# A recurrent stage with three gates of input first, one round ahead, and an ODE loop without work behind its branch

## The reference, cut to what matters

```python
def _mlp(y, W1, b1, W2, b2, W3, b3):
    h = jnp.tanh(y @ W1.T + b1)
    h = jnp.tanh(h @ W2.T + b2)
    return h @ W3.T + b3

def _rk4_step(y, dt, params):
    k1 = f(y)
    k2 = f(y + dt / 2 * k1)
    k3 = f(y + dt / 2 * k2)
    k4 = f(y + dt * k3)
    return y + dt * (k1 + 2 * k2 + 2 * k3 + k4) / 6
...
def _lstm_activate(gates, c):
    i, f, g, o = jnp.split(gates, 4, axis=-1)
    c_new = jax.nn.sigmoid(f) * c + jax.nn.sigmoid(i) * jnp.tanh(g)
    h_new = jax.nn.sigmoid(o) * jnp.tanh(c_new)
    return (h_new, c_new)

def step(carry, x_t):
    h, c = carry
    sel_in = jnp.concatenate([h, c, x_t], axis=-1)
    logits = sel_in @ W_sel.T + b_sel
    onehot = jax.nn.one_hot(jnp.argmax(logits, axis=-1), Sx, dtype=x_t.dtype)
    g_all = jnp.einsum('bi,sgi->bsg', x_t, W_ih) + jnp.einsum('bh,sgh->bsg', h, W_hh) + b_ih + b_hh
    g = jnp.einsum('bsg,bs->bg', g_all, onehot)
    h2, c2 = _lstm_activate(g, c)
    return ((h2, c2), h2)
```

## Time and profile before

| | us |
|---|---|
| median of 3 runs (lowest to highest) | 7168.47 (7166.38 to 7169.55) |
| the profiled execution | 7165.25 |
| its span | 7163.6 |
| PE busy over the span | 6236.3 (87%) |
| PEld busy | 4149.4 (58%) |
| DVE busy | 2602.1 (36%) |
| ACT busy | 1699.6 (24%) |
| POOL busy | 895.0 (12%) |

### The profile page before, as it was taken

One profiled execution on the slowest core, in us unless ns is written; L12 is line 12 of the kernel. 1 busy time (PEld: TensorE's weight loads), 2 busy tenths in 40 slices (PEclk: granted clock), 3 DMA queues, 4 the chain that ended last, 5 costly groups with the idle time before them and its releaser, 6 DMA issues. The chain is left out here.

```text
span 7163.6 us, 497293 instructions
## 1 busy us (share of the span) xinstructions
PE 6236.3 (87%) x212267; PEld 4149.4 (58%) x212267; DVE 2602.1 (36%) x12046; ACT 1699.6 (24%) x8390; POOL 895.0 (12%) x2042
## 2 busy tenths in 40 slices
PE   7857999999999999998789999999999999999831
PEld 5524555555555555554467777777777777777510
DVE  5324445454545211111233332333233332222267
ACT  0121333333333333333001111111111111111111
POOL 0011111111111584000000000000000000000000
PEclk9977999999999999999799999999999999999965
DMA  1011111111111110000232221222122211111100
GB/s 47 1 44 36 33 34 32 33 33 34 32 33 33 40 42 22 0 0 0 69 92 41 40 44 13 40 44 40 18 39 41 40 29 7 7 7 7 20 13 7
DMA packets 814786, 212.82 MB, mean 30 GB/s; under 512 B 706441, under 2 KB 772653, under 8 KB 814724
## 3 DMA queue, kind: packets, MB, share of 16 engines
q1 hardware_dynamic: 765700, 152.75, 11.1%
q0 software_dynamic: 47872, 54.13, 2.8%
q10 hardware_dynamic: 1152, 5.15, 0.2%
HBM read 183.50 MB, written 28.16 MB: 30 GB/s over the span
## 5 line engine op out<-in xcount | busy, mean ns | idle before, releaser
L1755 PE MATMUL ps_rows<-whh,h_pair 128*4 128x320 f16 x34944 | 1303.1, 299 | 85.7 <-issue 2.2
L1074 PE MATMUL ode_busy<-ode_busy_x,ode_busy_w 128*32 128x384 f16 (+4 forms) x18816 | 1253.8, 326 | 25.8 <-issue 14.8
L1755 PEld LDWEIGHTS ps_rows<-whh,h_pair 128*4 128x4 f16 x34944 | 739.9, 84 | 504.6 <-DVE h_pair L1613 155.7
L1068 PEld LDWEIGHTS ode_psa<-ode_a,ode_w2t 128*32 128x32 f32 x19968 | 421.5, 109 | 708.8 <-ACT ode_a L1181 562.8
L1625 DVE COPY gate_rows<-ps_rows_last 128x192 f32<-128x192 f32 x624 | 223.2, 358 | 1510.6 <-PE ps_rows_last L1755 1510.6
L1191 DVE SCALAR_TENSOR_TENSOR ode_part<-ode_b 128x1 f32<-128x1 f32 x624 | 110.6, 177 | 1608.1 <-ACT ode_b L1183 1608.1
L1677 ACT COPY gate_rows<-ps_rows 128x320 f32<-128x320 f32 x624 | 265.8, 426 | 1674.5 <-PE ps_rows L1755 1674.5
L1183 ACT ACTIVATE ode_b<-ode_psa 128x1 f32<-128x1 f32 x2496 | 427.4, 171 | 880.5 <-PE ode_psa L1068 880.5
L1068 PE MATMUL ode_psa<-ode_a,ode_w2t 128*32 128x1 f32 x19968 | 607.2, 180 | 1.0 <-issue 0.8
L1085 PE MATMUL ode_pso<-whh 125*32 125x170 f32 (+3 forms) x9600 | 564.3, 310 | 28.3 <-issue 28.3
L1799 PE MATMUL ps_gates<-l_gsel,gate_rows 128*32 128x4 f32 x19968 | 407.1, 177 | 137.9 <-DVE gate_rows L1625 128.5
(11 more groups left out here) (499 smaller groups left out, 9706.8 us busy)
## 6 DMA issues: line engine op xcount, KB each, us to landing
late_w<-in_wih_t SPq DMA_DIRECT2D x386, 128.0 KB, 2.1
xg_buf<-xg_scratch SPq DMA_DIRECT2D x1248, 16.0 KB, 2.0
split_raw<-in_whh_t SPq DMA_DIRECT2D x64, 256.0 KB, 2.6
ig_w<-in_wih_t SPq DMA_DIRECT2D x8, 2048.0 KB, 11.4
xg_scratch<-late_out SPq DMA_DIRECT2D x24, 624.0 KB, 3.2
whh<-h_scratch SPq DMA_DIRECT2D x105, 62.5 KB, 2.4
xg_scratch<-ig_out ACTq DMA_DIRECT2D x8, 628.0 KB, 8.0
h_scratch<-mlp_h SPq DMA_DIRECT2D x40, 125.0 KB, 2.3
```

What stands on the lines that cost most here:

```text
L1068: m = nc.tensor.matmul(ps[32 * j:32 * j + 32, 0:1], w[:, 32 * j:32 * j + 32], col, start=start, stop=stop, skip_group_check=True)
L1074: nc.tensor.matmul(ps_busy[32 * j:32 * j + 32, 0:cols], busy_w[:, 32 * j:32 * j + 32], busy_x[:, 0:cols], start=True, stop=True, skip_grou ...
L1755: m = nc.tensor.matmul(out[32 * j:32 * j + 4, :], hpair[:, c, 2 - 2 * part:6 - 2 * part], whh[:, at + lo:at + hi], start=(part == 0 and c ...
```

## The change

In the ODE SHADOW is UNITS + NT = 85, so that 85 iterations have message work and 71 don't. `job_slot` and the plain filler do nothing in slot 0; the pieces of the first half stand one slot later (1 to 6 and 7 to 9 in place of 0 to 5 and 6 to 8), which takes one busy slot away.

In the LSTM the rows of a cell are laid out by gate and not by column of each gate: a block of 512 holds 128 rows of each gate in the order input, candidate, forget, output (BLOCK_GATE), and the four matmuls of a group are the four blocks. `first` takes 384 columns, which are all of input, candidate and forget gate. The output gate's 128 come last, into a bank of their own (`ps_rows_out`). Ahead of the choice stands one block of `first` in place of two. Cells 0 to 2 have a bank each; cell 3 lies in the 128 columns that these three leave free, in three pieces. The input's share is added by two matmuls with the whole identity as weights, 12 columns for `ps_gates` and 4 for `ps_out_gate`. All 12 turns of the three gates stand behind ScalarE's copy, the 4 of the output gate behind VectorE's. ScalarE makes one tanh of 12 columns and then one of 4 (`out_gate_tanh`) ahead of `tanh_c`, and VectorE waits for this second one behind `c`, and then makes the output gate and weights the selector.

```diff
-SHADOW = 100
+SHADOW = UNITS + NT
...
-            if n < 6:
-                sum_piece(0, n // 3, n % 3)
-            elif n < 9:
-                weight_piece(1, n - 6)
+            if n == 0:
+                return
+            elif n < 7:
+                sum_piece(0, (n - 1) // 3, (n - 1) % 3)
+            elif n < 10:
+                weight_piece(1, n - 7)
...
-                    steps_tensor(pe, i, lambda n, cols: busy(cols), lambda r, s: None)
+                    steps_tensor(pe, i, lambda n, cols: busy(cols) if n else None, lambda r, s: None)
...
-    AHEAD = 2
-    FIRST = 5 * 64
+    FIRST = 3 * 128
+    IFG = 3 * KC
...
                     nc.vector.scalar_tensor_tensor(ccur, parts[:, KC:2 * KC], 0.5, parts[:, 0:KC], ALU.mult, ALU.add).then_inc(S["c_ready"], 1)
+                    v.wait_ge(S["out_acted"], k + 1)
+                    nc.vector.tensor_scalar(ok[:], out_tanh[:], 1.0, 1024.0, ALU.add, ALU.mult).then_inc(S["o"], 1)
+                    nc.vector.scalar_tensor_tensor(wgated[:], out_tanh[:].unsqueeze(2).broadcast_to([128, KC, PAIRS]), 1.0, wsel[:, 0:KC, :], ALU.add, ALU.mult).then_inc(S["w_ready"], 1)
...
-                    nc.vector.tensor_copy(gsb[:, FIRST:D], psb[:, 0:D - FIRST]).then_inc(S["evac_v"], 1)
+                    nc.vector.tensor_copy(gsb[:, FIRST:D], pso[:, 0:128]).then_inc(S["evac_o"], 1)
...
-                    nc.scalar.activation(act[:, 0:16], psc[:, 0:16], ACT.Tanh).then_inc(S["acted"], 1)
+                    nc.scalar.activation(act[:, 0:IFG], psc[:, 0:IFG], ACT.Tanh).then_inc(S["acted"], 1)
+                    a.wait_ge(S["out_gate"], k + 1)
+                    nc.scalar.activation(out_tanh[:], psq[:, 0:KC], ACT.Tanh).then_inc(S["out_acted"], 1)
...
-                        for c in range(AHEAD):
-                            for e in range(CELLS):
-                                first(e, 0, c)
+                        for e in range(CELLS):
+                            first(e, 0, 0)
...
-                            for j in range(4):
-                                m = nc.tensor.matmul(psc[32 * j:32 * j + 32, 0:16], ident[:, 32 * j:32 * j + 32], xgb[:, q, :, e * 8:(e + 1) * 8], start=True, stop=False, skip_group_check=True)
-                            m.then_inc(S["xg_used"], 1)
+                            nc.tensor.matmul(psc[:, 0:IFG], ident[:], xgb[:, q, e * 16:e * 16 + IFG], start=True, stop=False, skip_group_check=True)
+                            nc.tensor.matmul(psq[:, 0:KC], ident[:], xgb[:, q, e * 16 + IFG:(e + 1) * 16], start=True, stop=False, skip_group_check=True).then_inc(S["xg_used"], 1)
...
-                        turn(0)
-                        turn(1)
-                        turn(2, (0, 1))
-                        pe.wait_ge(S["evac_v"], k)
-                        turn(2, (2, 3))
-                        turn(3).then_inc(S["gates"], 1)
...
+                        turn(psc[:, 0:KC], 0, False)
+                        turn(psc[:, 2 * KC:3 * KC], 1, False)
+                        turn(psc[:, KC:2 * KC], 2, True).then_inc(S["gates"], 1)
+                        pe.wait_ge(S["evac_o"], k)
+                        turn(psq[:, 0:KC], 3, True).then_inc(S["out_gate"], 1)
+                        late(0)
+                        late(1)
```

More of the change, by code:

```diff
@@ L1538, in stage_lstm @@
         S = {k: new_semaphore(nc, "lstm_" + k) for k in (
-            "xg0_in", "init", "c_ready", "o", "w_ready", "h_made", "hp_ready", "logits", "best", "rows_first", "rows_last", "evac_a", "evac_v",
-            "gates", "acted", "fi", "tanh_c", "kept", "seen_v", "seen_a", "seen_g", "seen_pe", "xg_used", "late_used", "late_moved", "late_stored")}
+            "xg0_in", "init", "c_ready", "o", "w_ready", "h_made", "hp_ready", "logits", "best", "rows_first", "rows_out", "evac_a", "evac_o",
+            "gates", "out_gate", "acted", "out_acted", "fi", "tanh_c", "kept", "seen_v", "seen_a", "seen_g", "seen_pe", "xg_used", "late_used", "late_moved", "late_stored")}
         with nc.Block() as block:
@@ L1623, in step @@
                     v.sem_inc(S["seen_v"], 1)
[L1624 to L1625 removed]
+                    v.wait_ge(S["rows_out"], k)
+                    nc.vector.tensor_copy(gsb[:, FIRST:D], pso[:, 0:128]).then_inc(S["evac_o"], 1)
                     cell(k)
@@ L1749, in turn_of_two, with products @@
                         m.then_inc(S["logits"], 1)
-                        def products(e, part, c, out, lo, hi):
+                        def products(e, part, c, out, lo, hi, start):
                             for j in range(4):
@@ L1794, in turn_of_two, with turn, late @@
                                 recurrent(0)
[L1796 to L1812 removed]
+                        def turn(out, block_no, last):
+                            for j in range(4):
+                                m = nc.tensor.matmul(out[32 * j:32 * j + 32, :], gsb[:, block_no * 128 + 32 * j:block_no * 128 + 32 * j + 32], gsel[:, int(block_no == 1), :],
+                                                     start=False, stop=last, skip_group_check=True)
+                            return m
+                        def late(n):
+                            c = q * PER + n
+                            m = nc.tensor.matmul(ps_late[:, 0:BLOCK], late_w[:, c * 128:(c + 1) * 128], xt[:, c, ds(token, BLOCK)], start=(c == 0), stop=(c == KC - 1))
+                            if n == PER - 1:
+                                m.then_inc(S["late_used"], 1)
+                        pe.wait_ge(S["evac_a"], k)
+                        turn(psc[:, 0:KC], 0, False)
[5 more added lines that the diff above has]
+                        late(1)
                 assert LOOPS == (BLOCKS + 1) * TURNS
@@ L2218, in lay_out @@
     a["pairs"] = pairs.reshape(128, PAIRS)
-    gsel = np.zeros((128, 4), np.float32)
-    for j in range(4):
-        half = 1.0 if j == 2 else 0.5
-        gsel[32 * j:32 * j + 2, GATE_SLOT[j]] = half * 2.0 ** -17
-        gsel[32 * j + 2:32 * j + 4, GATE_SLOT[j]] = half * 2.0 ** -28
+    gsel = np.zeros((128, 2, KC), np.float32)
+    for j in range(KC):
+        for b, half in enumerate((0.5, 1.0)):
+            gsel[32 * j:32 * j + 2, b, j] = half * 2.0 ** -17
+            gsel[32 * j + 2:32 * j + 4, b, j] = half * 2.0 ** -28
     a["gsel"] = gsel
```

78 lines of the change are left out of this document (40 added, 38 removed).

## The result

The changed kernel takes 7233.95 us (median of 4 runs, 7231.08 to 7239.86) against 7167.43 us for the kernel before: a ratio of 1.0094, 95% interval 1.0077 to 1.0112. The profiled execution, the slowest of the four, took 7239.86 us with a span of 7238.2.

What follows compares the result with a forecast made beforehand. Chains of dependent steps in the ODE and LSTM were taken as the bound, not TensorE's busy time. 7165.25 - 51 (ODE) + 137 (LSTM) = 7251, with the median 3.2 higher 7254 us; range of this case 7205 to 7290.

Steps and rivals of the forecast that it cites:

- 6 of 11 us of clock falls: ODE, plain iterations: clock falls cost 11 us over all; the shorter gap behind the branch takes back 6, bounds 0 and 11.
- the sum: LSTM step, timed from the first chosen matmul: 0.22 us longer, bounds 0.15 to 0.26; 137 us more over 624 steps.
- factor of 1.12: LSTM, ScalarE's copy of 384 columns: 0.43 x 1.12 = 0.48 us, done at 1.86, hidden behind the identity.
- The mis-sized term: LSTM, from reduction to chosen cell: kept at 1.18 us, with 1.01 as lower bound.
- TensorE's route: LSTM, first chosen matmul to late matmuls: 2.62 us, before 2.33; 0.29 later, 0.26 after slack.
- step 5: LSTM, turns and late matmuls: turns end at 2.52, late matmuls at 2.62; TensorE's route 0.26 later, ScalarE's route 0.22.
- slack of 0.03: LSTM, logits: about 0.03 us of TensorE's route is slack, since the last logit matmuls wait for tanh_c today.
- ScalarE's route: LSTM, tanh of 12 columns starts at 2.67, where the tanh of 16 stood at 2.45: 0.22 us later.
- The range's upper end: Whole kernel, this case alone: 7290 us, the top of a range from 7205.
- Rival A: LSTM: identity passes slide under the copy of 384 columns; step 0.05 to 0.08 us shorter, 7073 us; chance 0.14.
- Rival B: LSTM: one shape change paid, or passes cheap as quarters; step 0.05 to 0.1 us longer, 7165 us; chance 0.09.
- Rival C: ODE: without the filler the clock falls behind most branches, 148 us more, 7453 us; chance 0.03.

Runs made afterwards that it cites:

- e4: The kernel before with the ODE part of the change alone: 7109.2 us, a ratio of 0.993.
- e11: The kernel before with SHADOW = 85 alone, the work behind the branch left where it was: 7169.13 us in a single run.
- e7: e6 with the input's share added by quarters of the identity in place of the whole identity: 7049.55 us, a ratio to before of 0.9846.
- e12: e7 with two blocks ahead of the choice for each of cells 0 to 2: 6956.61 us, a ratio to before of 0.9703.
- e2: The changed kernel with each of its two identity matmuls done twice: 7503.01 us in a single run.
- e10: The changed kernel with the ODE part of before: 7286.26 us, a ratio of 1.0163.
- e6: The changed kernel with cell 3 computed wholly behind the choice, in the bank of cell 0: 7230.3 us in a single run.
- e8: e7 with two more blocks of cell 1 ahead of the choice: 6879.78 us, a ratio to before of 0.9611.
- e9: The kernel before with one whole identity matmul in place of four quarters: 7166.24 us in a single run.
- e1: The changed kernel with the input's share added by quarters of the identity in place of the whole identity: 12766.35 us, a ratio of 1.783.
- e5: The changed kernel with 64 more matmuls in the branch of cell 3, ahead of its output gate: 12329.11 us in a single run.

## Why the prediction was right, and where its sizes were off

- **ODE.** Forecast 51 us less, bounds 30 and 58. By itself it gave 50 (e4); in the profile of the changed kernel its end came 58 us earlier. The terms per iteration hold: 17.49 with messages (the branch at L1223 came from 657.3 to 2388.5 in 99 turns) went to 17.21, 0.28 less, and the distance behind the branch is back at 0.53. One size was off: I took back 6 of 11 us of clock falls, and nearly all went, as 17.09 us for a plain iteration shows, where four ordinary steps of 4.27 make 17.08. The shorter first loop has no part in it (e11). Why falls are spared when nothing stands behind the branch is not shown: the rows tell that the iteration is shorter and that the clock of the plain loop is at 1.00, its upper level.
- **The 7 us** that came back in the input-gate stage were not forecast. They are not this execution's alone: from the last plain branch to the first reduction it is 285.5 us here (3319.7 to 3605.2), 286 in e7 and 288 in e12, but 279 in e2 and e4 and 278 in the kernel before. What decides it is not shown. So it is luck that the first reduction came 51 us earlier, just as much as was forecast for the ODE: it is 58 less 7.
- **LSTM.** Forecast 0.22 us a step, 137 in all; measured 0.202 and 126 in the profile, 119 by e10. The mechanism held step by step: identity's load 0.07 us before the last row's end, as forecast; 0.53 us until the turns (0.54 in the sum); ScalarE's copy, 0.48 long as in the sum (whose factor of 1.12 has no row behind it), done 0.38 before it is used; idling of 0.43 (0.4). The late matmuls start 2.60 us behind the first chosen rows (5002.92 to 5005.52; the sum had 2.62), and the logits 0.73 behind them, as before.
- **The mis-sized term** is the choice. The sum kept 1.18 us from reduction to chosen rows, with 1.01 as lower bound; it is 1.10. The rows of before gave 1.19, but there TensorE was busy with the work ahead until then; 1.10 is the choice by itself, with TensorE idling ahead of it (after, e6; 1.09 in e8). TensorE's route behind the chosen rows is 0.27 longer (2.60 against 2.33, 0.29 in step 5), the logits with the reduction behind them take 0.67 in place of 0.65, so that the slack of 0.03 in step 5 did not show, and the earlier choice takes 0.09 back: 4.90 to 5.10. That 0.22 came so near is in part luck: it was ScalarE's route in the sum, while TensorE's is the longer one, and the choice made up for the difference.
- The range's upper end does not follow from the bounds: 7168 - 30 + 162 is 7300, not 7290. The measured 7234 lies below both.
- **Rival A** (identity hidden, 7073 us) is out: e2 shows that its passes are paid in full, e7 that without it the step is 0.29 shorter. What e7 gives, 7050 us where before takes 7159, is what the rest of the change is worth when nothing holds up the turns. **Rival B** (0.05 to 0.1 us a step) is out too: the step is 0.20 longer. **Rival C** is out: the clock stood at 1.00 for the first 85 iterations, and in the plain loop as well.
- From the start of the last row to the first turn it is 0.68 us (5004.47 to 5005.15). Of these e2 prices the four passes at 0.112 each, 0.45 in all. The other 0.23 are the two waits for the change of shape, ahead of the identity (0.15) and behind it; they were not removed alone, so their own price is argued from the rows. Not all of the 0.68 is on the chain, since ScalarE's copy runs beside it: e7 starts the turns 0.33 us earlier against the copy's end, and its step is 0.29 shorter.

The Trainium skill, TensorEngine Tiling (Array Packing), Key Properties, says that a change of the tiling mode drains TensorE; the identity's load in this trace agrees, at 0.07 us before the end of the last quarter matmul, and the section gives no figure. The pulling of weight loads ahead of running matmuls, which the Trainium skill describes in TensorE: Matmul & The Clock Gate, section on the array as 16 sub-arrays, is seen among the quarters (the loads of `ps_rows_out` start 0.16 us ahead of their matmuls, 5003.91 and 5004.07) and not across that change.

## What to carry to other kernels

Before you shorten a wait, list what stands in its shadow: the four quarters made no difference while VectorE's copy was on the chain (e9), and became worth 0.29 us of each step as soon as it was not (e7). Here, among matmuls that use a quarter of the array, the full-width ones on the chain cost their passes (0.112 us each) and, as argued above, a wait on either side. And an idle engine ahead of a decision is not a loss by itself: fill it with work that shortens what comes behind (e8, e12), not with work for its own sake.

## What the hardware showed that was not expected

The loop's code has a length beyond which each turn loads it again. A turn of the LSTM's loop holds two tokens. Counted in the program's text (two records, weights and matmul, for an f16 matmul and four for an f32 one), turns of 1624 records (e2) ran with 36 packets on the instruction queue in the whole program; turns of 1752 (e1) and 1816 (e5) had 2809 and 2836 packets of some 16.4 KB (46.02 MB / 2809), and the mean step went from 5.1 to (12304.0 - 3594.7) / 623 = 13.98 and (11884.8 - 3598.2) / 623 = 13.30 us. Code that is hardly ever executed counts as well: the padding of e5 stands in a branch that 6 of 624 steps take. Part of the longer step is the clock: over the whole of these two runs the granted clock was 0.68 and 0.69, and a matmul of `ps_rows` took 442 ns on average in e1 against 300 in the changed kernel. How much of the loss is the idling and how much the clock was not separated. The Trainium skill, Runtime: NRT & Kernel Launch, section on instruction fetch mechanics, says that instructions come in blocks of 16 KiB; the packet size in these runs agrees. The same section of the Trainium skill says that a taken branch out of what is held forces a fetch; no run here shows what a single branch does.
